# Two-layer tower with a Mamba layer: both parts of a softplus step size move to the end of VectorE's unit

## The reference, cut to what matters

```python
xn = _layer_norm(x, g, b)
xs, z = jnp.split(xn @ in_w, 2, axis=-1)              # 512 channels each
xc = silu(causal_conv4(xs) + conv_b)
delta = jax.nn.softplus(xc @ xd_w @ dtp_w + dtp_b)    # the step size
Bm, Cm = xc @ xB_w, xc @ xC_w                         # 16 states
dA = jnp.exp(delta[..., None] * A)
dBx = (delta * xc)[..., None] * Bm[:, :, None, :]
h = dA_t * h + dBx_t;  y = sum over states of h * C_t # scan over 257 tokens
y = y + D * xc
return y * silu(z) @ out_w + res
```

## Time and profile before

| | us | share of the span |
|---|---|---|
| median of 3 runs | 10189.29 | |
| the profiled execution | 10188.56 | |
| its span | 10186.8 | |
| PE busy | 8303.1 | 82% |
| DVE busy | 8072.5 | 79% |
| POOL busy | 7033.7 | 69% |
| ACT busy | 5908.9 | 58% |

### The profile page before, as it was taken

How to read it: one execution, slowest core, us unless ns; L and a number is a source line. 1 busy time by engine, 2 the same in 40 slices (tenths; PEclk the granted TensorE clock), 3 DMA queues, 4 the chain that set the end, 5 groups by cost and what they waited for, 6 DMA issues and landing times. The chain is left out here.

```text
span 10186.8 us, 153042 instructions
## 1 busy us (share of the span) xinstructions
PE 8303.1 (82%) x42776; PEld 6791.3 (67%) x42776; DVE 8072.5 (79%) x10482; ACT 5908.9 (58%) x9234; POOL 7033.7 (69%) x7227
## 2 busy tenths in 40 slices
PE   5888878787878788878888878787878776999998
PEld 4666666666666666666666666666666664777776
DVE  4999989898989898989898989898989993333332
ACT  4666666666666666666666666666666662544443
POOL 4888888888888888888888888888888882000000
PEclk8888888888888888888888888888888887999999
DMA  3222222222222222222222222222222220000000
GB/s 95 96 91 100 94 100 93 97 96 98 95 99 88 98 94 98 94 100 94 85 92 85 93 98 96 98 96 94 98 96 98 94 84 24 11 12 8 12 9 10
DMA packets 414835, 818.80 MB, mean 80 GB/s; under 512 B 148918, under 2 KB 194138, under 8 KB 414042
## 3 DMA queue, kind: packets, MB, share of 16 engines
q1 hardware_dynamic: 410328, 806.69, 23.2%
q10 hardware_dynamic: 3714, 2.89, 0.1%
HBM read 783.16 MB, written 26.30 MB: 79 GB/s over the span
## 5 line engine op out<-in xcount | busy, mean ns | idle before, releaser
L787 ACT ACTIVATE decay<-delta,neg_a 128x512 f32<-128x512 f32 x4096 | 2801.1, 688 | 2429.4 <-DVE h_ps L991 1119.7
L548 POOL TENSOR_TENSOR bu<-b_all,u_buf 128x512 f32<-128x512 f32 x3072 | 3573.6, 1189 | 110.4 <-DVE h_ps L991 107.1
L991 DVE TENSOR_TENSOR_SCAN h_ps<-decay,bu 128x512 f32<-128x512 f32 x2304 | 2776.8, 1222 | 594.6 <-ACT decay L787 504.8
L1249 PE MATMUL y_ps<-ident,ch 128*128 128x128 f32 x16384 | 2492.1, 301 | 555.5 <-DVE ch L1011 450.1
L1249 PEld LDWEIGHTS y_ps<-ident,ch 128*128 128x128 f32 x16384 | 2115.3, 155 | 935.5 <-DVE ch L1011 618.6
L560 POOL TENSOR_TENSOR ch<-ch,c_all 128x512 f32<-128x512 f32 x1024 | 1326.4, 1295 | 1036.5 <-DVE ch L991 868.8
L1011 DVE TENSOR_TENSOR ch<-h_ps,c_all 128x512 f32<-128x512 f32 x3072 | 1975.8, 670 | 0.0
L1134 PE MATMUL w_ps<-xn,in_w 128*128 128x257 f32 x4096 | 1123.2, 422 | 179.1 <-ACT xn L676 61.1
L551 POOL TENSOR_TENSOR bu<-b_all,u_buf 128x514 f32<-128x514 f32 x1024 | 1252.3, 1244 | 12.7 <-DVE h_ps L991 12.3
L995 DVE TENSOR_TENSOR_SCAN h_ps<-decay,bu 128x256 f32<-128x256 f32 x1536 | 1048.3, 737 | 62.8 <-POOL bu L551 38.2
L1134 PEld LDWEIGHTS w_ps<-xn,in_w 128*128 128x128 f32 x4096 | 829.8, 213 | 357.3 <-issue 67.2
(11 more groups left out here) (262 smaller groups left out, 11466.9 us busy)
## 6 DMA issues: line engine op xcount, KB each, us to landing
b_all<-bc_dram SPq DMA_DIRECT2D x512, 514.0 KB, 6.5
c_all<-bc_dram SPq DMA_DIRECT2D x512, 514.0 KB, 7.5
in_w<-in_L_attn_in_w SPq DMA_DIRECT2D x64, 1024.0 KB, 5.0
diag_store<-diag_dram SPq DMA_DIRECT2D x256, 256.0 KB, 3.5
x_in<-in_x SPq DMA_DIRECT2D x128, 256.0 KB, 3.8
out_w<-in_L_attn_out_w SPq DMA_DIRECT2D x64, 512.0 KB, 3.9
skip_diag<-skip_dram SPq DMA_DIRECT2D x64, 256.0 KB, 4.1
h_mid<-h_cur SPq DMA_DIRECT2D x32, 257.0 KB, 2.1
```

The costliest lines, as they stand in the source:

```text
L548: pool.tensor_tensor(bu[:, s % NBU, 0:NB * L].rearrange("p (b t) -> p b t", b=NB), b_all[:, n // NU, n % NU, :, 1:], u_buf[:, c % 2, :, 1: ...
L787: func(decay[:, s % NDP, :].rearrange("p (b t) -> p b t", b=NB), delta[:, c, :, 1:S], ACT.Exp, scale=neg_a[:, k, c, n:n + 1]).then_inc(dec ...
L991: dve.tensor_tensor_scan(h, decay[:, s % NDP, :], bu[:, s % NBU, 0:NB * L], 0.0, ALU.mult, ALU.add).then_inc(scan_done, 1)
L1249: last = pe.matmul(y_ps[:, k, :], ch[:, s % NPR, k * P:(k + 1) * P], ident[:, :], is_transpose=True, start=False, stop=(n == NST - 1 and k ...
```

## The change

In each unit with a step size, part 0 no longer stands between the unit's two scans; it stands behind the products with C, directly ahead of part 1. The numbers and kinds of instructions stay the same on every engine, and no engine's order but VectorE's changes.

```diff
                     if jj == 4 and u in (6, 8):
                         merged(g, (u - 6) // 2)
-                    if size:
-                        step_size(*size, 0)
                     scan(g, jj, s + 1, 0)
                     if s + 1 in POOL_C and s < NST:
                         c_times_h(g, jj, s)
...
                         if s + 1 not in POOL_C:
                             c_times_h(g, jj, s + 1)
                     if size:
+                        step_size(*size, 0)
                         step_size(*size, 1)
                     if u == 1 and not first:
                         output(g, jj - 1, 3)
```

## The result

| | before | after |
|---|---|---|
| median, us | 10189.16 (4 runs: 10188.9 to 10202.66) | 10268.8 (4 runs: 10263.41 to 10278.41) |
| ratio, 95% interval | | 1.0075 [1.0063, 1.0088] |
| the profiled execution | 10188.56 | 10278.41 |
| its span | 10186.8 | 10276.7 |
| granted clock, mean of the span | 0.884 | 0.888 |

The change makes the kernel slower, by 80 us. The forecast was 52 us slower (10241), and its range ended at 10262, 7 us under the measured median. The direction and the mechanism held; a part of the loss was not in the sum. The profiled execution of after was the highest of its four, 9.6 us over their median, so a sum over its trace explains 90 us, not 80.

The account below looks back on a forecast made before the run. Neither VectorE's scans nor ScalarE's decays, each waiting for the other, had backlog to absorb a shift. 42 us at seams plus 10 us in jobs made +52 us on 10189.29, forecast 10241 us, range 10195 to 10262.

Parts of the forecast that it names:

- the price of a step: VectorE step-size instructions: about 0.66 us with GpSimd silent, otherwise the rest of GpSimd's instruction plus 0.55.
- who goes next: Two VectorE instructions with both inputs in SBUF in a row: a waiting GpSimd instruction goes between them.
- Rival 1: VectorE keeps its turn, GpSimd doesn't slip between part 0 and part 1: -54 us, 10135; chance 8%.
- Rival 2: Only one of the bad collisions in units 31 and 2 comes: no change, 10190 to 10198 or 10177; chance 8%.
- the gap of 0.03: Between part 0 and part 1 on VectorE, overlap turns into a 0.03 us gap, losing about 0.11 us.
- rival 4: Part 1's wait for part 0 inside the loop is dear: slower still, 10287; chance 4%.
- the local sum: 0.67 us at 63 seams between jobs plus 0.15 in 64 jobs (units 2 and 3): +52 us.
- This chain moves by the whole 0.67: Next job's start: decays, `y_t` copy, TensorE's turn and VectorE's `sz` product shift by the full 0.67 us.
- the 0.90 us of unit 3: Unit 3: part 0 no longer falls into GpSimd's sum, gaining 0.90 us per job.
- I count every local shift in full: Assumption for the job loop: a VectorE delay at a job's start moves the rest of that job.
- rival 3: The shift is absorbed later in the job: no change to +0.2%, 10215 if half is lost; chance 10%.
- The second phase has none of this: The kernel's second phase contributes nothing to the +52 us.

Follow-up runs that it names:

- a plain delay: Kernel before plus one, two or three unread VectorE reductions behind part 1 of unit 31, step sizes untouched: 10231.27, 10248.53 and 10263.87 us.
- unit 2 alone: Kernel before with part 0 moved behind the products in unit 2 only: 10193.74 against 10193.85 us, ratio 1.0000.
- only unit 2 or 3 moved: Two kernels, each the kernel before with part 0 moved in one unit: unit 2 10193.74 us, ratio 1.0000; unit 3 10195.36 us, ratio 1.0002.
- the changed kernel with the filler: Changed kernel plus 20 unread identity products on TensorE in the fourth job's 3.3 us wait: 10249.37 against 10193.56 us for the kernel before, ratio 1.0055.
- Unit 30 alone: Kernel before with part 0 moved behind the products in unit 30 only: 10158.19 us, ratio 0.9969.

## Why the prediction was wrong in size

**Right: the price of a step.** Undisturbed about 0.68 us, otherwise the rest of GpSimd's instruction plus 0.55. The durations forecast for after and those measured, in the stretches above: `diag_store` 0.67 and 1.4 (0.67 and 1.40), `sp_l` 1.7 and 0.68 (1.65 and 0.69), `sq` 0.68 and 1.45 (0.68 and 1.48), `cen` 0.68 and about 1.5 (0.69 and 1.47). The largest error is 0.05.

**Right: who goes next.** The argument from a single pair decided the sign, and held in every job. Rival 1, VectorE keeping its turn, would have shown part 1 on `sp_l` at 0.66 in unit 2; it has 1.65, so it falls. Rival 2 falls too, since both collisions came in every job.

**Right: the gap of 0.03.** Part 0 of unit 2 ends at 3057.81 and part 1 starts at 3057.84, part 0 of unit 3 ends at 3063.86 and part 1 starts at 3063.89. So the wait by a register is no dearer than the lead-in's, and rival 4 falls. The rule of the Trainium skill (page "VectorE: DVE Perf Modes", section "The DRAIN you can't avoid") that a semaphore between VectorE operations costs nothing extra, which the page measured on a row of copies, doesn't agree with this trace: the pitch of an undisturbed pair is 0.70 or 0.71 us, where an instruction of 0.66 without such a wait has one of 0.58.

**Right: the local sum.** Forecast 0.67 us per seam, measured 0.65 to 0.67 behind jobs 1 to 3. Forecast 0.15 us per head, measured 0.17 in the first job and 0.09 in the others, a term of 10 us that measured 6.5. The missing 0.06 us is close to what a plain delay loses in the heads of the same jobs (0.07 to 0.09), so the step "This chain moves by the whole 0.67" is off by about that. One step of it was booked to the wrong edit: the 0.90 us of unit 3 come from unit 2's delay, as the kernel with unit 2 alone shows. A forecast for one of these units by its own term would have been wrong by about 1 us a job.

**Wrong: "I count every local shift in full".** This was the assumption on which all rested, and I only asked whether less than the full shift would arrive (rival 3). Less than a tenth of a us per job was absorbed, so rival 3 falls, and the jobs lost more besides. The failed step is the silent half of the assumption, that the middle of a job keeps its length when its start moves. It didn't: TensorE's clock fell in scans 24 to 28 of job 4, in eight groups of 15, and in scans 16 to 20 in all 15, where it never had in before. That is 21 and 9 us in the profiled run, offset in part by jobs 1 to 3, for +22 us in all middles. The delays show that the shift does it by itself, with 11 to 20 us over what was left of their length. The profile of before had what was needed to see the risk: the wait of 3.3 us on TensorE stands in it, and the granted clock can be read for each stretch. I read neither in job 4, since no instruction of the change runs on TensorE. What it could not show is where the clock would fall after a shift; a wider range was what it could have given.

**Missing: the jump at the loop's end.** The sum had no term for VectorE's branch behind job 4, because it was hidden. It costs 7 us in after, and why it got longer stays open. The sign of such a term could not be told from before; that there is a branch right behind the moved instructions could.

**"The second phase has none of this."** The stretch behind the last scan was 11.4 us longer in the profiled run. In the kernels with only unit 2 or 3 moved, whose totals equal before's, it was 10.8 and 7.1 longer. So I don't put it down to the change. TensorE's time at the lower clock in that stretch goes along with its length: 197 us in before, 226 in after (+11.4), 225 and 218 with unit 2 or 3 moved (+10.8, +7.1), and 191 in the changed kernel with the filler (-2.8). What moves it there stays open.

Summed on the medians: 54 us of heads and seams (47 forecast terms, 7 the jump), and 26 more, of which the middles' 22 of the one profiled run are the part with a place. The other 4 have no owner; the interval of the ratio spans 25 us. That heads, seams and the middles of one run come this near to 80 us is in part luck.

**A better version.** Unit 30 alone: 10158.19 us, ratio 0.9969 [0.9959, 0.9979], faster than both kernels. It takes the one place of the four in which the move by itself leaves one collision where there were two.

## What to carry to other kernels

An instruction with both inputs in SBUF on VectorE or GpSimd is to be placed by what the other engine does in that microsecond: two of them in a row on VectorE, with GpSimd queued, cost two of GpSimd's instructions, and one product with an operand in PSUM between them frees the pair. When all jobs get longer or shorter by a few tenths, ask as well what TensorE's clock does in the middle of the job: list the stretches in which TensorE waits for some microseconds and then is waited for, read their granted clock, and put the difference between the two levels into the range on both sides. Look at every such wait: filling one left the lower clock at the next. Judge a local reordering at each of its places alone; here four places gave 0, 0, -36 and +96 us, and the sum hid the one worth keeping.

## What the runs showed of the hardware

- **A shift elsewhere moves the lower clock.** With jobs 0.3 us longer by a plain delay, a 12 us stretch went to up to 15.2, at a granted clock of 0.78 where it was 1.00. The mean clock of the whole span says nothing of this: after has 0.888, before 0.884, and after is slower.
- **More work, less time.** Twenty idle matmuls in a wait of 3.3 us made the changed kernel 19 us faster and left the kernel before unchanged. The lower clock stayed away behind that wait and showed more often at an earlier one.
- **The two engines alternated in every place.** Where a GpSimd instruction was waiting, it went between two of VectorE's that have both inputs in SBUF (units 2 and 31, 127 places in after), and VectorE's second ended 0.55 us behind it.
- **The price of a loop's branch isn't fixed.** On VectorE it was 0.53 us and hidden, or 1.2 to 2.7 us and partly exposed (0.2 to 1.5 us), for the same loop with one or both parts 0 moved at its end. The Trainium skill (page "Runtime: NRT & Kernel Launch", section "Instruction fetch mechanics") says that a taken branch whose target isn't at hand stalls until its page is fetched; no run here shows whether that is what is seen.
